# Macaron layer on Trainium2: V and the keys loaded in four parts, spread over the steps of a block

## The reference

```python
q, k, v = x @ Wq, x @ Wk, x @ Wv                  # 16 heads of 64
k, v = 4 memory rows ahead of the 1024 keys / values
dots = einsum('bhid,bhjd->bhij', l2norm(q), l2norm(k)) * 10
dots = einsum('hg,bgij->bhij', W_pre_th, dots)    # heads are mixed
dots = causal mask; keep the 64 largest of each row, mask the rest
attn = softmax(dots)
attn = einsum('hg,bgij->bhij', W_post_th, attn)   # heads are mixed again
out = einsum('bhij,bhjd->bhid', attn, v) * head_scale * sigmoid(x @ Wg + bg)
return out @ Wo
```

## Time and profile before

| | |
|---|---|
| median of three runs | 3582.88 us |
| the profiled execution | 3581.46 us, its span 3578.9 us |
| PE busy | 3160.2 us (88%) |
| DVE busy | 2552.0 us (71%) |
| ACT busy | 2523.4 us (71%) |
| POOL busy | 2016.8 us (56%) |
| granted TensorE clock, mean | 0.943 |
| DMA queue of SyncE | 363048 packets, 461.62 MB, 43.8% of 16 engines' span |

### The profile page before, as it was taken

One profiled execution on the slowest core, in us unless ns is written; L12 is line 12 of the kernel. 1 busy time (PEld: TensorE's weight loads), 2 busy tenths in 40 slices (PEclk: granted clock), 3 DMA queues, 4 the chain that ended last, 5 costly groups with the idle time before them and its releaser, 6 DMA issues. The chain is left out here.

```text
span 3578.9 us, 73640 instructions
## 1 busy us (share of the span) xinstructions
PE 3160.2 (88%) x23206; PEld 2089.0 (58%) x23206; DVE 2552.0 (71%) x6406; ACT 2523.4 (71%) x5857; POOL 2016.8 (56%) x6011
## 2 busy tenths in 40 slices
PE   7999999996788998888899887899988889988998
PEld 4444444443556666656666665566676566667566
DVE  4444444444788998678998867899986889986354
ACT  3444454443788999688999967889986888896222
POOL 1221221223787767687776767776777877674332
PEclk9999999996799999989999989999997999999899
DMA  3222222225466664355666345666534556642010
GB/s 129 94 90 104 106 106 94 83 82 173 141 179 179 185 181 98 108 155 173 185 183 157 90 119 151 179 179 186 144 88 130 166 178 181 181 108 74 12 36 30
DMA packets 363531, 467.11 MB, mean 131 GB/s; under 512 B 29476, under 2 KB 295204, under 8 KB 362664
## 3 DMA queue, kind: packets, MB, share of 16 engines
q1 hardware_dynamic: 363048, 461.62, 43.8%
HBM read 227.18 MB, written 234.36 MB: 129 GB/s over the span
## 5 line engine op out<-in xcount | busy, mean ns | idle before, releaser
L1142 ACT ACTIVATE junk<-D,nt 128x76 int8<-128x76 f32 (+62 forms) x1440 | 1070.4, 747 | 98.9 <-POOL nt L1230 65.2
L1047 PE MATMUL banks<-kr,E 128*128 128x128 f32 (+1 forms) x4672 | 707.0, 300 | 106.4 <-ACT AT L1165 60.7
L1047 PEld LDWEIGHTS banks<-kr,E 128*128 128x128 f32 (+1 forms) x4672 | 605.6, 203 | 256.7 <-issue 154.2
L1020 PE MATMUL banks<-Sg,kpre 128*128 128x109 f32 (+51 forms) x1568 | 605.1, 494 | 22.9 <-POOL maskb L1299 13.0
L1372 DVE COPY Sn<-banks 128x686 f32<-128x686 f32 (+11 forms) x440 | 375.5, 853 | 176.2 <-PE banks L1007 145.0
L1397 DVE SCALAR_TENSOR_TENSOR W<-SG,sgn,W 128x76 f32<-128x76 int8 (+14 forms) x480 | 412.8, 899 | 103.4 <-POOL W L1252 102.9
L1006 PE MATMUL banks<-kT,qT 64*128 64x343 f32 (+11 forms) x880 | 395.8, 532 | 101.9 <-DVE Sn L1372 95.9
L1165 ACT ACTIVATE AT<-banks 128x512 f32<-128x512 f32 (+3 forms) x768 | 345.2, 479 | 195.6 <-PE banks L1047 194.5
L1075 PE MATMUL banks<-AT,V 128*64 128x64 f32 x9216 | 394.1, 233 | 87.6 <-issue 75.4
L1075 PEld LDWEIGHTS banks<-AT,V 128*64 128x64 f32 x9216 | 324.2, 143 | 162.6 <-issue 143.1
L1462 DVE SCALAR_TENSOR_TENSOR E<-D,vk,E 128x12 f32<-128x12 f32 (+56 forms) x512 | 394.8, 780 | 3.1 <-ACT E L1152 1.5
(11 more groups left out here) (197 smaller groups left out, 5253.9 us busy)
## 6 DMA issues: line engine op xcount, KB each, us to landing
score_scratch<-Sn SPq DMA_DIRECT2D x96, 343.0 KB, 3.3
v_scratch<-a_share SPq DMA_DIRECT2D x32, 512.0 KB, 3.6
q_scratch<-a_share SPq DMA_DIRECT2D x32, 512.0 KB, 2.8
k_scratch<-a_share SPq DMA_DIRECT2D x32, 512.0 KB, 2.8
gate_scratch<-a_share SPq DMA_DIRECT2D x32, 512.0 KB, 2.7
kT<-k_scratch SPq DMA_DIRECT2D x32, 512.0 KB, 5.0
gateT<-gate_scratch SPq DMA_DIRECT2D x32, 512.0 KB, 10.2
qT<-q_scratch SPq DMA_DIRECT2D x31, 512.0 KB, 6.4
```

What stands on the lines that cost most here:

```text
L1020: out = nc.tensor.matmul(bank[:, 0:c], kpre[:].rearrange("p h r -> p (h r)"), Sg[:, g % 3, c0:c1], start=True, stop=not diagonal)
L1047: out = nc.tensor.matmul(ps[5 + i % 2][0:rows, c % 4 * P:(c % 4 + 1) * P], E[:, g % 4, c * P:c * P + rows], kr[:, g % 4, :], start=True, s ...
L1142: nc.scalar.activation(out, D[:, e, 1:1 + n], ACT.Sign, bias=nt[:, r, e:e + 1], scale=-1.0, accum_out=cnt[:, r, e:e + 1]).then_inc(s[f"cnt ...
```

## The change

`keys` and the new function `keep` (the V part of the old `late`) take a list of parts. Of the next block but one, the keys that were loaded whole at the end of step 6 are loaded one quarter (two of the eight head pairs, all 128 partitions) at the end of each of steps 0 to 3. The V rows of the block, which were loaded whole at the end of step 7, are loaded one quarter at the end of each of steps 2 to 5: 31 rows each, and with the last part the four rows for the next chunk. For the first block of a batch, whose region of `kT` or `V` is still being read, both stay together: the keys at the end of step 6 in four parts, V at the end of step 6 in four parts. Queries stay at the end of step 6, gates at the end of step 7. The waits count four landings for the keys, five for V.

```diff
-            def keys(G):
+            def keys(G, parts_=range(PARTS)):
                 b, ib = G // IB, G % IB
                 if b >= 1:
                     sp.wait_ge(s["s_ps"], UC[b * IB])
                     sp.wait_ge(s["kmean"], b * IB)
-                sp.dma_start(kT[:, :, 1 + MEM + ib * P:1 + MEM + (ib + 1) * P],
-                             kd[b, :, :, ib * P:(ib + 1) * P]).then_inc(s["k_in"][G % 2], 16)
+                for c in parts_:
+                    pairs = slice(c * HP // PARTS, (c + 1) * HP // PARTS)
+                    sp.dma_start(kT[:, pairs, 1 + MEM + ib * P:1 + MEM + (ib + 1) * P],
+                                 kd[b, :, pairs, ib * P:(ib + 1) * P]).then_inc(s["k_in"][G % 2], 16)
...
-            def late(G):
+            def keep(G, parts_):
                 b, ib, r = G // IB, G % IB, G % IB * P
                 if b >= 1:
                     sp.wait_ge(s["av"], 2 * IB * b)
-                sp.dma_start(V[MEM:P, ib, :], vd[b, r:r + P - MEM, :]).then_inc(s["v_in"][G % 2], 16)
-                sp.dma_start(V[0:MEM, ib + 1, :], vd[b, r + P - MEM:r + P, :]).then_inc(s["v_in"][G % 2], 16)
+                for c in parts_:
+                    lo, hi = c * (P - MEM) // PARTS, (c + 1) * (P - MEM) // PARTS
+                    sp.dma_start(V[MEM + lo:MEM + hi, ib, :], vd[b, r + lo:r + hi, :]).then_inc(s["v_in"][G % 2], 16)
+                if PARTS - 1 in parts_:
+                    sp.dma_start(V[0:MEM, ib + 1, :], vd[b, r + P - MEM:r + P, :]).then_inc(s["v_in"][G % 2], 16)
+
+            def late(G):
+                b, r = G // IB, G % IB * P
                 if G >= 1:
                     sp.wait_ge(s["y"], G)
...
                 if 2 * k + 4 < NT:
                     load(2 * k + 4)
+                if G + 2 < NB and (G + 2) % IB and k % 8 < PARTS:
+                    keys(G + 2, [k % 8])
                 if k % 8 == 6 and G + 2 < NB:
-                    keys(G + 2)
+                    if (G + 2) % IB == 0:
+                        keys(G + 2)
                     queries(G + 2)
+                if G < NB and G % IB and 2 <= k % 8 < 2 + PARTS:
+                    keep(G, [k % 8 - 2])
+                if G < NB and G % IB == 0 and k % 8 == 6:
+                    keep(G, range(PARTS))
                 if k % 8 == 7 and G < NB:
                     late(G)
...
-                        pe.wait_ge(s["k_in"][G % 2], 16 * (G // 2 + 1))
+                        pe.wait_ge(s["k_in"][G % 2], 16 * PARTS * (G // 2 + 1))
...
-                        pe.wait_ge(s["v_in"][G % 2], 32 * (G // 2 + 1))
+                        pe.wait_ge(s["v_in"][G % 2], 16 * (PARTS + 1) * (G // 2 + 1))
```

More of the change, by code:

```diff
@@ L998, in units @@
                     if u == 0:
-                        pe.wait_ge(s["k_in"][G % 2], 16 * (G // 2 + 1))
+                        pe.wait_ge(s["k_in"][G % 2], 16 * PARTS * (G // 2 + 1))
                         if G == 1:
-                            pe.wait_ge(s["k_in"][0], 16)
+                            pe.wait_ge(s["k_in"][0], 16 * PARTS)
                         pe.wait_ge(s["q_in"], 16 * G)
@@ L1357, in key_mean @@
                 else:
-                    dve.wait_ge(s["k_in"][(G - 1) % 2], 16 * ((G - 1) // 2 + 1))
+                    dve.wait_ge(s["k_in"][(G - 1) % 2], 16 * PARTS * ((G - 1) // 2 + 1))
                     lo = 1 + MEM + (ib - 1) * P
```

## The result

The changed kernel takes 3813.79 us in the median of four runs (3807.97 to 3821.37), the kernel before 3577.96 us in the runs beside it; the ratio is 1.0683, 95% interval 1.0655 to 1.0711. It is 6.8% slower, 236 us.

What follows compares the result with a forecast made beforehand. VectorE, TensorE and ScalarE, busy side by side in the attention stage, were taken as the bound, not DMA. Waits of 275 us, less 80 absorbed and 8 relief, plus 3 start, gave +190 on 3581.46: median 3773 us, range 3625 to 3960.

Steps and rivals of the forecast that it cites:

- 31 rows go to one engine: V's parts: 31 being prime, each part goes to a single DMA engine, always the same, where 124 rows use four.
- rival 1: V's parts spread over four engines or more, 1.7 us or less each, so nothing waits: 3578 us, chance 7%.
- A part holds its engine 6.0 us: Each V part occupies its one engine 6.0 us, as long as whole V did four, delaying the transfers issued next.
- Keys cost nothing: Keys cut in four and moved to steps 0 to 3 still use 16 engines: cost 0, bounds 0 to 48 us.
- Waits at stores, 187 us gross in 60 places: Score copies wait for stores behind V's parts, steps 3 to 5 of blocks 2 to 6: 15.6 us times three times four.
- Waits at row loads, 88 us gross: Mixes wait for row loads behind V's parts: tile 15 48 plus 16 us, block 1's steps 2 to 4 24 us.
- The first block of a batch: In four blocks V comes one step earlier, counted within the -8 us gain of moving V out of step 7.
- DMA transfers hold up almost nothing: In the kernel before, earlier or smoother loads could win back about 20 us in all, in 28 places.
- Absorption: Idle VectorE time in the steps makes up part of the 275 us gross waits: 80 us taken, 130 at most.
- Rival 2: One engine is clogged, but VectorE and TensorE do other work and catch up: 3600 to 3640 us, chance 10%.
- rival 3: Spreading the 1.5 MB burst of steps 6 and 7 helps the next block's tiles: at most 20 us, 3563 us, 3%.
- Rival 4: Backlog carries over between steps in blocks 3 to 6, each part costing 6 us or more: over 3965 us, 5%.

Runs made afterwards that it cites:

- experiment 3: The changed kernel with V's four parts cut at 32, 32, 32 and 28 rows instead of 31 each: 3538.97 us, ratio 0.9883 to the kernel before.
- experiment 4: The changed kernel with V's four parts cut by columns, all 124 rows by 256 columns each: 3551.2 us, ratio 0.9915 to the kernel before.
- experiment 7: The kernel before, keys whole, with V in four 31-row parts issued together at its old place, step 7: 3970.49 us, ratio 1.1087.
- experiment 8: The kernel before, keys whole, with V in two pieces of 112 and 12 rows at its old place, step 7: 3525.4 us, ratio 0.9851.
- experiment 11: The kernel before with V uncut but issued one step earlier, at the end of step 6 ahead of keys and queries: 3638.67 us, ratio 1.017.
- experiment 9: The changed kernel with V in parts of 31, 48 and 45 rows (first block of a batch 48, 32, 44): 3639.44 us, ratio 1.0188 to the kernel before.

## Why the prediction was right, and where it was not

The prediction was +190 us by one mechanism, measured are +236 us, inside the range, and the mechanism is shown. Two of its terms had the wrong sign or size and nearly cancel, which is luck.

- *31 rows go to one engine:* right. The share of 0.07 and the updates of V's semaphore show it directly, experiments 3, 4 and 7 by its effects. The Trainium skill, "DMA: Bandwidth & Descriptors", section "Why a DMA increments its semaphore by 16 and not by 1", says how many engines k a transfer gets from the outer sizes of its two sides: issuing "picks the largest k ≤ 16 that divides both of those dim sizes". The traces agree for 124, 112, 62, 45, 32, 31, 28 and 12 rows (4, 16, 2, 15, 16, 1, 14 and 12 engines); rival 1 is out.
- *A part holds its engine 6.0 us:* nearly right. In the stretch at the end of block 8 it is 5.1 us a part; the 6.0 were worked out from four engines at 21 GB/s each.
- *Keys cost nothing:* right, slightly pessimistic. They gained 0.3% alone, and nothing beside experiment 8's V.
- *Waits at stores, 187 us gross in 60 places:* measured 162.8 us in 63 places, of which 159 us in 58 places are in steps 3 to 5 of blocks 2 to 6, where the prediction put them. The sizes by block were more even than thought: 3.0, 2.9, 2.7, 2.6 and 2.0 us a step in blocks 2 to 6 in the mean, where 3.2, 3.0, 3.0, 1.6 and 4.8 were taken. The single copies that were walked measured 4.83, 2.11 and 3.36.
- *Waits at row loads, 88 us gross:* 209.8 us. The places that the term took were sized well: tile 15 has 75 us (64 taken), tiles 9, 11 and 13 of block 1 have 22.5 (24 taken). What it left out is tile 1 of the second block of each batch, four long waits of 15.3 to 17.1 us, 66.4 us together, and tile 9 of blocks 2 to 5, 24 us. Experiment 3 has 13.7 us of such waits anyway.
- *The first block of a batch:* this is the step that failed most plainly. The prediction put there a gain ("in four V comes one step earlier", in the -8 us) and left out that its four parts are issued in a row, so that one engine is held four times as long. Measured: a loss of 42 us (3813.8 - 3772.1).
- *"DMA transfers hold up almost nothing":* this failed too. It was read from the waits that the profile books to a DMA, and two of its numbers, 8.7 and 3.2 us, are the same waits on TensorE's two rows. V's landing is not told, and TensorE's waits for V stood under "issue" on the values line, which the prediction did not list: 75.4 us besides the 4.2. V's four engines were taken as busy for 8 to 9 us from its issue; its last landing came after 9.5 to 12.6 us. Without V's hold the kernel is 38 us (experiment 3) to 53 us (experiment 8) faster than before, against the -8 taken and the -20 given as its bound. How much of the 53 is the wait for V itself and how much the gates and loads behind it is not separated: experiment 11 took the first away and made the second worse.
- *Absorption:* gross waits of 275 us, 80 of them absorbed, 195 net, stood for the parts in the steps. The changed kernel's waits beyond experiment 3's are 196 us at row loads and 153 at stores, 349 in all, and 275 us are the whole difference between the two kernels. That looks like a fifth absorbed, where three tenths had been taken, but the comparison does not measure absorption: the 275 us also hold TensorE's busy time, 115 us longer in the changed kernel's profile than in experiment 3's (3246.7 against 3131.8) with the same matmuls. The prediction had no term for a slower TensorE clock behind the waits. How much of the 115 us lies on the path that sets the time is open, so more than a fifth may have been absorbed.

The sum against the measurement, by differences of medians: parts in the steps +233 (195 taken), first blocks +42 (0), relief and start together -38 (-5); 237 in all. The misses in the second and third term, +42 and -33, nearly cancel by luck; that in the first, +38, is what is left. Rival 2 (absorbed, 3600 to 3640 us) and rival 3 (a gain by spreading) are out. Step 7 did have something to win, as rival 3 said, but it was V's hold on four engines and not the burst: cutting V at 112 rows where it stands gives all of it. (The transfers of steps 6 and 7, keys, queries, V and gates, are 2.0 MB together; rival 3 said 1.5.) Rival 4's saturation did not come: the time stayed below 3965 us, and the waits behind the second and third part of a block (51 and 68 us) are smaller than behind the first (105 us), so no backlog grew from step to step.

Why a lone part cost 3.6 us (experiment 9) and each of four 2.1: most of it is the place. In the changed kernel the first parts have 105 of the 299 us of waits behind the four. By that share of the 233 us a first part costs 2.9 us, an estimate. Whether the rest comes from parts that follow each other was not tried, as no run has a lone part at another place.

The version to keep is experiment 8: two pieces of 112 and 12 rows in V's old place, 3525.4 us, 1.5% faster than before and 7.6% faster than the changed kernel.

## What to carry to other kernels

Before cutting a transfer, look at the number of rows of each piece: the number of engines it gets can be read from the DMA share of a stretch in which it runs alone. A piece of 31 rows, a prime number above 16, took one engine for about as long as the whole of 124 rows took four. Choose cuts at multiples of 16, also where a transfer is not cut today: 124 rows on four engines cost this kernel 1.5%. A transfer's price is what stands behind it in the queue, so place it by who is issued next. Read "issue" waits on a line that uses loaded data as possible waits for that load when the profile gives the load no landing. Do not add the two rows of TensorE.

## What the runs showed of the hardware

- An issue on SyncE is not always short. With four 31-row parts on one engine, the next issue, of four rows, took 4.76 us and a later one 8.50 us (rows of SyncE above). The 4.76 us came in the first block of all four batches, against 0.29 to 0.37 us for the same four rows in the other 28 blocks. Issuing itself waited; that it waited for the filled queue of the one engine is the likely reading, not tested.
- TensorE's clock fell with the waits. In the 15 us of the long wait at the end of block 0 the row of the changed kernel reads, with TensorE busy 1.88 us of them:
```profile
890.00:905.00 15.00, 1.88 (x7) 1.52 (x7) 3.30 (x21) 5.14 (x24) 6.59 (x31) 0.50 0.25 75
```
  A granted clock of 0.50 is the level of 1.2 GHz. The mean over the kernels goes with their time: 0.951 at 3525 us, 0.943 before, 0.913 for the changed kernel, 0.896 for experiment 7. The 86.5 us by which TensorE's busy time rose with the same matmuls fit work at a lower clock after a wait. Here is the same matmul right behind the long wait of block 8 and 6 us later, at a granted clock of 0.50 and of 1.00 in the stretches around it:
```profile
1570.47 1.01 PE L1021 MATMUL banks<-kT,qT 64*128 64x389 f32 x1
...
1576.51 0.59 PE L1021 MATMUL banks<-kT,qT 64*128 64x389 f32 x1
```
